# Last pair's sums from the exponentials, inverse on VectorE, four PSUM banks for its out-projections, and small weights kept on chip

## What is computed

```python
x = x + 0.5 * ffn(layernorm(x), ...)
x = x + attn(layernorm(x), ...)
x = x + 0.5 * ffn(layernorm(x), ...)

# attn: inner layernorm with scale and bias, latents of 128, 16 heads of 64
q = (c_q @ w_up_q.T).reshape(b, s, H, DH).transpose(0, 2, 1, 3)      # k and v from c_kv, q and k rotated
attn = softmax(q @ k.T * scale, axis=-1)
out = (attn @ v).transpose(0, 2, 1, 3).reshape(b, s, H * DH) @ w_out.T + residual

# ffn: 8 experts and a shared one, hidden width 128, top 2 by sigmoid(x @ gate_W)
h = gelu(einsum('bsd,edh->bseh', x, W1) + b1)
y = einsum('bseh,ehd->bsed', h, W2) + b2
out = einsum('bse,bsed->bsd', gate_full, y) + shared
```

## Time and profile before

| | us |
|---|---|
| median of 3 runs | 4242.8 (4238.97 to 4249.39) |
| profiled execution | 4230.41 |
| its span, first to last instruction | 4228.6 |
| its mean granted TensorE clock | 0.984 |
| busy: PE, PEld | 3947.9 (93%), 2236.5 (53%) |
| busy: DVE, ACT, POOL | 2965.4 (70%), 2772.1 (66%), 3032.1 (72%) |

### The profile page before, as it was taken

The page is one execution under the profiler, slowest core; times in us unless marked ns, Lnnn a source line. Parts: engine busy times, 40 slices in busy tenths (PEclk is TensorE's granted clock), DMA queues, the critical chain, the costliest instruction groups (busy, mean ns, idle before and its releaser), DMA issues. The chain is left out here.

```text
span 4228.6 us, 66236 instructions
## 1 busy us (share of the span) xinstructions
PE 3947.9 (93%) x24896; PEld 2236.5 (53%) x24896; DVE 2965.4 (70%) x3707; ACT 2772.1 (66%) x3536; POOL 3032.1 (72%) x1642
## 2 busy tenths in 40 slices
PE   7999979999999999999999999999999999779999
PEld 6888834444444444444444444444444444368888
DVE  5556568777777777777777777777777877455663
ACT  4454457777777776777777777777777777644544
POOL 3444458878888887888888788878887888734444
PEclk9999989999999999999999999999999999989999
DMA  3333221112111211121112112111211122133331
GB/s 107 108 121 111 73 90 61 52 54 82 53 51 59 76 54 57 55 71 52 60 59 68 61 51 72 59 53 56 81 51 51 63 70 62 36 99 116 121 111 61
DMA packets 194224, 301.08 MB, mean 71 GB/s; under 512 B 51470, under 2 KB 102256, under 8 KB 193264
## 3 DMA queue, kind: packets, MB, share of 16 engines
q1 hardware_dynamic: 193904, 296.86, 21.9%
HBM read 201.86 MB, written 26.74 MB: 54 GB/s over the span
## 5 line engine op out<-in xcount | busy, mean ns | idle before, releaser
L1037 DVE TENSOR_REDUCE atNM<-atPS 128x2 f32<-128x1024 f32 x1024 | 1208.0, 1220 | 558.0 <-PE atPS L854 552.7
L1126 POOL TENSOR_TENSOR atACC<-atACC,atPT 128x1024 f32<-128x1024 f32 x512 | 1286.6, 2513 | 69.5 <-ACT atPT L975 15.7
L975 ACT ACTIVATE atPT<-atPS 128x1024 f32<-128x1024 f32 x1024 | 995.8, 1022 | 196.3 <-PE atPS L875 187.8
L886 PE MATMUL atPO<-atPT,atV 128*64 128x512 f32 x4096 | 972.5, 595 | 0.0
L966 ACT ACTIVATE atPS<-atSH 128x1024 f32<-128x1024 f32 x768 | 767.4, 1022 | 37.7 <-DMA atSH<-atMD 22.8
L1126 POOL TENSOR_TENSOR atACC<-atPT 128x1024 f32<-128x1024 f32 x256 | 621.7, 2429 | 107.6 <-PE atOT L897 104.4
L854 PE MATMUL atPS<-atKH,atQH 64*128 64x512 f32 x2048 | 456.5, 448 | 123.8 <-ACT atPT L975 112.2
L1105 POOL TENSOR_TENSOR atVT<-atVT,atSIN 128x512 f32<-128x512 f32 x254 | 332.4, 1309 | 296.6 <-DMA atVT<-atR 296.4
L886 PEld LDWEIGHTS atPO<-atPT,atV 128*64 128x64 f32 x4096 | 282.1, 137 | 474.0 <-issue 467.2
L875 PE MATMUL atPS<-atQH,atKL 64*128 64x512 f32 x2048 | 468.7, 454 | 36.4 <-ACT atPS L966 33.2
L875 PE MATMUL atPS<-atQH,atKH 64*128 64x512 f32 x2048 | 406.3, 392 | 0.0
(11 more groups left out here) (276 smaller groups left out, 6817.3 us busy)
## 6 DMA issues: line engine op xcount, KB each, us to landing
atSH<-atMD SPq DMA_DIRECT2D x128, 512.0 KB, 4.3
atVT<-atR SPq DMA_DIRECT2D x508, 128.0 KB, 2.0
f1GB<-f1GD SPq DMA_DIRECT2D x128, 256.0 KB, 6.8
atRSUM<-atRD SPq DMA_DIRECT2D x128, 256.0 KB, 4.0
f2GB<-f2GD SPq DMA_DIRECT2D x128, 256.0 KB, 6.9
X<-x SPq DMA_DIRECT2D x4, 1024.0 KB, 5.8
XS<-x SPq DMA_DIRECT2D x16, 256.0 KB, 3.9
atRQ<-atRSUM SPq DMA_DIRECT2D x256, 4.0 KB, 1.8
```

The lines of the kernel that those rows point to most:

```text
L886: ins = pe.eng.matmul(PO[HI[h], :], V[n % 2][:, j, HI[h]], PT[k % NPT][:, h, :], start=j == 0, stop=j == T - 1)
L975: act.eng.activation(PT[k % NPT][:, :, :], PS[ring.of[step]][:, :, :], ACT.Exp, scale=SCALE).then_inc(grown.sem)
L1037: dve.eng.tensor_reduce(NM[:, q // 4, :, q % 4, t], PS[ring.of[step]][:, :, :], AX.X, ALU.max, negate=True).then_inc(most_out.sem)
L1126: pool.eng.tensor_tensor(total[:, :, :], begun[:, :, :], PT[k % NPT][:, :, :], ALU.add).then_inc(gathered.sem)
```

## The change

In the last pair of heads (n = NN - 1) the sums are made in another way. Half 0 uses the two gathered sums, accumulated in PSUM; half 1 uses the one gathered sum of key blocks 0 to 3 and the four exponentials of blocks 4 to 7 directly, so GpSimd's three gathers of those are left out. The matmuls use 64 columns of ones, so each sum arrives on all 64 partitions of its head. VectorE takes the reciprocal of 128 x 512 values from PSUM and multiplies AT with it; the copy on ScalarE, the column layout, the trip through HBM and GpSimd's divide of this pair go. Its four out-projections lie in four banks of `PS` and don't wait for each other.

The attention no longer waits for its last stores at its end; the second FFN's SyncE does, behind its loads of W1 and W2 (`held`). gWp, b2s, sel, desc, rsc and b1 are allocated outside the blocks, so the second FFN does not load or prepare them again. In both FFNs b2's rounding now stands ahead of W2's instead of behind it.

The diff, cut to its core:

```diff
+    gWp = ctx.enter_context(nc.sbuf_tensor("gWp", [128, 2, 128], fp32r))
+    b2s = ctx.enter_context(nc.sbuf_tensor("b2s", [GK, D], fp32r))
+    sel, desc = (ctx.enter_context(nc.sbuf_tensor(x, [n, E], fp32)) for x, n in (("sel", 2 * E), ("desc", 128)))
+    rsc, b1 = (ctx.enter_context(nc.sbuf_tensor(x, [128, n], fp32)) for x, n in (("rsc", 1), ("b1", NE)))
...
                     elif name == "w2":
-                        act.wait_ge(*seconds(1))
+                        act.wait_ge(*seconds("w2"))
+                        if not second:
+                            act.eng.activation(b2s[:, :], b2f[:, :], ACT.Copy).then_inc(act_w.sem)
                         act.eng.activation(W2h[:, :], W2f, ACT.Copy).then_inc(act_w.sem)
-                        act.eng.activation(b2s[:, :], b2f[:, :], ACT.Copy).then_inc(act_w.sem)
...
-                if not first_done:
+                if not second:
                     load(0)
-                for x, name in ((ident, "ident"), (gWf, "gate"), (sel, "sel"), (rsc, "rs"), (desc, "desc"), (b1, "b1")):
-                    sp.eng.dma_start(x[:, :], a[name]).then_inc(small.sem, 16)
+                    for x, name in ((ident, "ident"), (gWf, "gate"), (sel, "sel"), (rsc, "rs"), (desc, "desc"), (b1, "b1")):
+                        sp.eng.dma_start(x[:, :], a[name]).then_inc(small.sem, 16)
                 sp.eng.dma_start(W1f, a["W1"]).then_inc(firsts.sem, 16)
+                if not second:
+                    sp.eng.dma_start(b2f[:, :], a["b2"]).then_inc(seconds.sem, 16)
                 sp.eng.dma_start(W2f, a["W2"]).then_inc(seconds.sem, 16)
-                sp.eng.dma_start(b2f[:, :], a["b2"]).then_inc(seconds.sem, 16)
+                for sem, count in held:
+                    sp.wait_ge(sem, count)
                 for b in range(1, NX):
                     load(b)
...
-                at(end, m, 19, ("invert", m))
-                at(end, m, 20, ("inverse", m))
-                at(end, m, 21, ("broadcast", m))
-                at(begin, m, 23, ("divide", m, 0), ("divide", m, 1))
+                if m < NN - 1:
+                    at(end, m, 19, ("invert", m))
+                    at(end, m, 20, ("inverse", m))
+                    at(end, m, 21, ("broadcast", m))
+                    at(begin, m, 23, ("divide", m, 0), ("divide", m, 1))
...
-            other_before.update(zip(others[13:], others[12:]))
+            other_before.update(zip(others[13:-4], others[12:]))
+            room.update({use: PS[i // 2][:, i % 2, :] for i, use in enumerate(others[-4:])})
...
                     elif name == "sum":
                         _, n, t = step
                         free(step)
+                        pe.wait_ge(*made(1))
+                        if n == NN - 1:
+                            pe.wait_ge(*gathered(n, t, 3 if t else T - 1))
+                            parts = [ACC[acc(n, t, half)] for half in range(2 - t)]
+                            if t:
+                                pe.wait_ge(*grown(n, t, T - 1))
+                                parts += [PT[((2 * n + t) * T + j) % NPT] for j in range(4, T)]
+                            for x, part in enumerate(parts):
+                                for h in range(2):
+                                    ins = pe.eng.matmul(OT[HI[h], :], ones[:, :], part[:, h, :], start=x == 0, stop=x == len(parts) - 1)
+                            ins.then_inc(summed.sem)
+                            continue
                         pe.wait_ge(*gathered(n, t, T - 1))
...
-                        pe.wait_ge(*divided(n, u // 2))
+                        if n < NN - 1:
+                            pe.wait_ge(*divided(n, u // 2))
+                        else:
+                            pe.wait_ge(*grown(n, 1, T - 1))
+                            pe.wait_ge(*divided(n - 1, u // 2))
+                            pe.wait_ge(*ended(u // 2, "divided"))
...
+                    elif name == "sum" and step[1] == NN - 1:
+                        _, n, t = step
+                        sums, o = (x[:, t * 512:(t + 1) * 512] for x in (RSUM[n % 2], AT[:, n % NAT, :]))
+                        dve.wait_ge(*summed(n, t))
+                        dve.wait_ge(*divided(n - 2, t))
+                        dve.eng.reciprocal(sums, OT[:, :]).then_inc(ended.sem)
+                        dve.wait_ge(*ended(t, "inverse"))
+                        dve.wait_ge(*attend_out(n, t))
+                        dve.eng.tensor_tensor(o, o, sums, ALU.mult).then_inc(ended.sem)
...
-                for u in range(4):
-                    sp.wait_ge(*stored[u](NB - 1))
 
             launch(tensor, scalar, vector, gpsimd, sync)
+            return [stored[u](NB - 1) for u in range(4)]
```

More of the change, by code:

```diff
@@ L142, in prepare @@
             def prepare(b):
-                normed = [s and (s[0], b, 0, s[1]) for s in once()] if b or not first_done else []
+                normed = [s and (s[0], b, 0, s[1]) for s in once()] if b or not second else []
                 picks = [("pick", b, i) for i in range(8)]
@@ L150, in after @@
                 again = [s and (s[0], NB, r, s[1]) for r in range(2) for s in once()]
-                return [None] * (2 * LAG + 2) + [("next", 0), None, None] + again if norms_after else []
+                return [None] * (2 * LAG + 2) + [("next", 0), None, None] + again if not second else []
             order, first = [], prepare(0)
@@ L234, in tensor @@
                         bank = wides[take(wide, step)]
-                        if b or not first_done:
+                        if b or not second:
                             pe.wait_ge(*normed(b, 0))
-                        pe.wait_ge(*small(5))
+                        pe.wait_ge(*small.past(5))
                         for i in range(4):
@@ L561, in sync @@
                         sp.eng.dma_start(X0[:, :, :], rows(dst, 0)).then_inc(fetched.sem, 16)
-                for b in range(NB - NX, NB - 1 if norms_after else NB):
+                for b in range(NB - NX, NB - 1 if not second else NB):
                     sp.wait_ge(*stored[b % NX](b))
             launch(tensor, scalar, vector, gpsimd, sync)
-            return stored[(NB - 1) % NX](NB - 1)
+            return [stored[(NB - 1) % NX](NB - 1)]
     def launch(tensor, scalar, vector, gpsimd, sync):
@@ L697, in attention @@
                 order += begin.get(g, []) + scores + mosts + early.get(g, []) + fills + attends
-                order += [("gather",) + s[1:] for s in attends if s[3] % 4] + late.get(g, []) + end.get(g, [])
+                order += [("gather",) + s[1:] for s in attends if s[3] % 4 and s[1:3] + (s[3] // 4,) != (NN - 1, 1, 1)] + late.get(g, []) + end.get(g, [])
             def events(*names):
@@ L747, in attention @@
             broadcast = sig("broadcast", 32).expect(heads)
+            ended = sig("ended").expect([(t, x) for t in range(2) for x in ("inverse", "divided")])
             divided = sig("divided").expect(halves)
@@ L982, in scalar @@
                             act.eng.activation(AT[:, n % NAT, t * 512:(t + 1) * 512], PO[:, :], ACT.Copy).then_inc(attend_out.sem)
[L983 removed]
+                    elif name == "sum" and step[1] < NN - 1:
                         _, n, t = step
@@ L1137, in sync @@
                     sp.eng.dma_start(x[:, :], a[name]).then_inc(outs.sem, 16)
-                sp.wait_ge(*last_stored)
+                for sem, count in held:
+                    sp.wait_ge(sem, count)
                 for u in range(4):
```

75 lines of the change are left out of this document (40 added, 35 removed).

## The result

| | before | after |
|---|---|---|
| median | 4240.9 (4238.8 to 4249.4, 4 runs) | 4208.4 (4204.8 to 4209.7, 4 runs) |
| ratio, 95% interval | | 0.9918 (0.9901 to 0.9935) |
| profiled execution | 4230.41 | 4204.82 |
| its span, granted clock | 4228.6, 0.984 | 4202.9, 0.986 |

Against the median of 4242.8 that stood ahead of the forecast, 24.7 us were forecast; 32.5 us were gained (4240.9 - 4208.4). The sign and the mechanism were right, the size was a quarter short, and 4208.4 lies at the very low end of the range. The two profiled executions differ by 25.6 us only. The windows, then the timeline of the changed kernel, show the forecast part of the gain first. Windows of after: the same two as in the earlier trace rows.

A forecast was written before the change was run, and what follows sets the result against it. An 80 us hole from attention to second FFN, where TensorE is not the bound, delays a TensorE-bound stage. 20.5 + 3.8 + 0.4 = 24.7 us off the 4242.8 median gives 4218.1, range 4208 to 4229.

The forecast's parts named there:

- 1, first half's sum: Last pair's first sum on TensorE, in 64-column strips: 1.94 us instead of 1.06, costing 0.88 us.
- 2, second half's sum, from the last attend: Last pair's second sum, 20 instructions straight from the exponentials, following the attends without a gap: 4.28 us.
- 3, inverse: VectorE's reciprocal of 128x512 from PSUM, extrapolated from three smaller sizes on one line: 3.35 us.
- 4, multiply: 128x512 multiply replacing the copy, eight DMAs and GpSimd's divide: 0.69 us, as for an add, up to 1.42.
- 5, last attend to last add: Attention's exit, out-projections in four banks: last add at 3692.7 instead of 3711.44, 18.7 us gained; 13 us instead of 32.5.
- 6, last add to first DMA: Block end without waiting for stores: 0.87 us instead of 2.63 to the second FFN's first DMA; 20.5 us gained so far.
- 7, choice into the block: Second FFN's head without small loads, W1 now late: choice of experts at 11.0 us instead of 14.83, 3.8 gained.
- 8, choice to the turn of batch 1: b2 kept, so W2's low part starts sooner on GpSimd: 0.4 us gained, ends 0 and 0.8.
- A: Rival: the second FFN's head gives nothing back, W1's landing or ScalarE's order takes it; 20.5 us gained, 4222; chance 0.12.
- B: Rival: TensorE's low clock comes anyway, two exit out-projections cost about 3 us more; 21.7 gained, 4221; chance 0.05.
- C: Rival: kept tiles shift the attention's buffers, slower reads in the 63 earlier pairs; a 0.3% loss means 4256; chance 0.03.
- D: Rival: old waits covered something that now shows, or scatter; less than 12.7 us gain remains, about 4235; chance 0.08.

The follow-up runs named there:

- a_again: The changed kernel (after) run once more, unchanged: 4208.4 us, ratio 0.9923 to before.
- a_wait: After with the wait for the last stores back at the attention's end: 4211.2 us, +2.4 ± 3.7 against after.
- h_head: Before with no wait for stores at the attention's end, small tiles kept outside the blocks and b2 ahead of W2, without the exit: 4229.3 us, ratio 0.9973.
- x_exit: Before with the new exit alone (sums, inverse, four banks), keeping the wait for the stores and the small loads: 4225.7 us, ratio 0.9959.
- b_same: Before against itself, nothing changed: ratio 1.0008 (0.9997 to 1.0019).
- n_pad: Before with one unused tile of 2152 bytes a partition allocated ahead of all others: 4243.7 us, ratio 1.0006.
- n_shift: Before with gWp, b2s, sel, desc, rsc and b1 only allocated outside the blocks, all instructions the same: 4236.2 us, ratio 0.9985.
- n_shift2: Second run of n_shift, before with the same tiles only allocated outside the blocks: 4237.6 us, ratio 0.9993.
- b_al64: Before with every SBUF tile starting on a multiple of 64 bytes: mean 4233.4 us, ratio 0.9984.
- a_onebank: After with the last four out-projections in a single PSUM bank again: 4213.9 us, +5.8 ± 2.6 against after.
- a_split: After with the second half's inverse and multiply in two parts of 256 columns: 4205.1 us, ratio 0.9915 to before.
- v2: After with a new order in the FFNs' heads and the second inverse and multiply in two halves: 4197.2 us, ratio 0.9907 to before.
- v2_al64: v2 with every SBUF tile on a multiple of 64 bytes: 4196.8 us, ratio 0.9902 to before.
- a_gap64: After with an unused 64-byte gap ahead of each FFN's weight tiles, which stay on a multiple of 64: mean 4212.1 us, ratio 0.993 to before.
- a_mis: After with the four weight tiles W2h to W1l put 32 bytes off a multiple of 64: mean 4221.5 us, ratio 0.9962 to before.
- a_misw1: After with only W1h and W1l put 32 bytes off a multiple of 64: mean 4223.2 us, ratio 0.9959 to before.

## Why the prediction was right, and where it was wrong

| step | forecast | measured, in the one profiled execution of after |
|---|---|---|
| 1, first half's sum | 1.94 instead of 1.06 | 1.89 |
| 2, second half's sum, from the last attend | 4.28 | 4.29 |
| 3, inverse | 3.35 | 3.36 |
| 4, multiply | 0.69 | 0.69 |
| 5, last attend to last add | 13 | 12.97 |
| 6, last add to first DMA | 0.87 | 0.79 |
| 7, choice into the block | 11.0 | 11.04 |
| 8, choice to the turn of batch 1 | -0.4 | -0.47 |
| other pairs and both FFNs | 0 | about -7 |

**What held.** In that profile steps 1 to 8 came out within 0.1 us each, since each took its duration from a row and each was placed in the chain before it was added. For the head this is in part luck: in a_again step 7 is 12.53. The reciprocal is the clearest: three points on a line, 153 + 6.25 n, gave 3.35 us at eight times the largest size seen, and line L1089 took 3.36. The rule weighed there (the Trainium skill, VectorE: DVE Perf Modes, "First, the fixed hardware budget": a repeat count of 8 for the reciprocal) would by the prediction's estimate have had 4.4; the measurement speaks against that estimate. W1 became the late one in the head, as said, and the queue behind the moved wait for the stores cost nothing: a_wait changes the boundary and not the choice.

**The step that failed** is the sentence "The pairs before the last and the rest of both FFNs issue the same instructions: 0". The instructions are the same; their operands are not where they were. The six tiles moved outside put the FFN's weight tiles, which had started 32 bytes off a multiple of 64, onto one. Worked out from the shortest batches: 7 x 0.44 us in each of the two FFNs and 0.6 for the last batch is 6.8 us. The batches with a stretch of low clock, on the mean over the kernels of each sort, give 0.37 instead of 0.44, and so 5.8. The alignment alone gives 7.0 ± 2.6 in before, and its loss costs 13.1 and 14.8 in after, where 14 batches lose 0.7 us each and the last one 1.0, 10.8 together. The halves agree: h_head, which moves the tiles, gained 10.8 where 6.0 were forecast, and x_exit, which moves none, 16.4 of 18.7. For the pairs of heads the zero was right.

A smaller share lies in the step that priced the exit. It took before's exit from one profile, 38.72 us from first sum to last add. In seven profiles with that exit (before, b_same, n_pad, n_shift, n_shift2, h_head, b_al64) it takes 37.8 to 41.1, 39.7 on the mean, and 20.03, give or take 0.01, in every profile with the new one, a_onebank, a_split, v2 and v2_al64 aside. So the exit is worth some 19.6 us instead of 18.7. 24.7 + 0.9 + 5.8 = 31.4, against 32.0 ± 2.6 measured.

**The rivals.** A did not come: the head gave its 3.8 us. B did not come in the exit: its out-projections ran at the upper level, and the four banks left TensorE no idle time over 0.82 us before the boundary; a_onebank shows what B would have looked like. In the head the low level did come, and it cost a_again most of the 1.5 us above, on matmuls that B did not name. Nor did D. C asked the right question, whether moved tiles are read at another speed, and looked for the answer in one place only, the exponentials of the earlier trace rows, which indeed don't feel it. It had the sign of a loss alone; the trace of before could have given neither sign nor size for the FFN's matmuls, but 0 there was a choice and needed bounds on both sides. One percent of the two FFNs' some 1040 us, either way, would have widened the range by 10 us on both sides.

**Why the profiles hid it.** In before's profiled execution the second FFN had 11.3 us of low granted clock from the turn of batch 1 on, in after's 21.3. A batch that holds one such stretch of 3.4 us takes some 1.4 us more (on the mean 61.3 instead of 59.9 in the kernels placed as before, 60.9 instead of 59.5 in those placed as after), so three stretches more cost about 4 us, which ate the 3 us that the FFN gained there, and the profiled pair agreed with the forecast by chance. The stretches themselves don't go with the place of the tiles: they lie in 32 of 48 batches of the first sort and in 101 of 144 of the second, the last batch of each FFN aside. Only batches of one kind, compared kernel by kernel, showed the step.

## What to carry to other kernels

Price an exit from the durations of its rows and lay it out as a chain: eight steps summed this way were right to 0.1 us each in one profile. Take the stretch that is to go from several profiles, since the same exit of before took 37.8 to 41.1 us. Then ask of a change not only what it issues but which tiles it moves: here an allocation alone was worth 0.1 to 0.2% with no instruction changed, so an edit of this size needs a control that only allocates. And compare a repeated unit that no disturbance touched (the shortest batch), since single executions scatter by more than such an effect.

## What the runs showed of the hardware

- The start of the FFN's weight tiles modulo 64 bytes changes the time of its matmuls: 389 ns against 394 for f2XH with f2W1l, 392 against 394 for f2XL with f2W1h, and 47.44 against 48.40 us for the last batch, in a_gap64 and a_mis with 32 bytes between the two places. Matmuls that don't read the misplaced tile slow down as well (W2h with GH, 280 against 283 ns in a_misw1), so it is not the operand's own start alone that counts. The attention showed nothing of the kind (3139 to 3149 us up to the last pair's first sum).
- Stretches of low granted clock come in the midst of a steady FFN, too, behind full work: in the 14.2 us ahead of the one at 3874.3 us in after, TensorE was busy for 14.20 at a clock of 1.00, and the clock was 0.50 in the 3.4 us behind. There are 2 to 6 of 3.4 us between the turn of batch 1 and the last microseconds, differing between executions; what brings them is open. Executions of before lie between 4225.5 us (mean granted clock 0.985) and 4255.9 (0.978).
- The reciprocal on VectorE is linear in its elements from 8 to 512: 203, 253, 553 ns, 1.76 us for 256 and 3.36 us for 512.
